# Dummy TensorE products around the first expert unit, and a reordered square root in the tail, in an LSTM-step + MoE block

## The reference, cut to what matters

```python
def step(carry, xp_t):                       # 8 steps, one after the other
    h_prev, c_prev = carry
    g = xp_t + h_prev @ u                    # 512x128 @ 128x512
    gates = sigmoid(g[:, :3 * H]); c_cand = tanh(g[:, 3 * H:])
    ...
    c = fg * c_prev + ig * c_cand
    h = og * tanh(c)
...
x = layernorm(x + lstm(x))
logits = einsum('GSM,ME->GSE', x, router_w)          # 8 groups of 512 tokens, 8 experts
dispatch, combine = gating_top2(logits, C=128)
expert_inputs = einsum('GSEC,GSM->EGCM', dispatch, x)
hidden = gelu(expert_inputs @ w0) * (expert_inputs @ w1)   # 128 -> 688
expert_outputs = hidden @ wo                               # 688 -> 128
x = layernorm(x + einsum('EGCM,GSEC->GSM', expert_outputs, combine))
```

## Time and profile before

| what | value |
|---|---|
| median of 3 runs | 311.33 us (310.96 to 311.38) |
| the profiled execution's own time | 310.78 us |
| its span | 309.0 us |
| mean granted clock of TensorE | 0.979 |
| busy share of the span: PE, DVE, ACT, POOL | 91%, 83%, 69%, 57% |

### The profile page before, as it was taken

The page is one execution under the profiler, slowest core; times in us unless marked ns, Lnnn a source line. Parts: engine busy times, 40 slices in busy tenths (PEclk is TensorE's granted clock), DMA queues, the critical chain, the costliest instruction groups (busy, mean ns, idle before and its releaser), DMA issues.

```text
span 309.0 us, 5728 instructions
## 1 busy us (share of the span) xinstructions
PE 279.8 (91%) x1671; PEld 233.7 (76%) x1671; DVE 257.9 (83%) x816; ACT 213.5 (69%) x484; POOL 176.7 (57%) x148
## 2 busy tenths in 40 slices
PE   8999988975969999999999999999999999897840
PEld 8666555635968999999998787788888888787730
DVE  2789997899859998888888988988777678899975
ACT  4787865556687777776778687776655665564964
POOL 5011148878777787776878578827447265662400
PEclk9999999977999999999999999999999999999995
DMA  6996081724273227224454857524223135452444
GB/s 193 379 395 238 8 253 48 217 69 134 78 225 92 71 69 228 65 57 52 72 93 35 204 71 164 71 20 64 45 25 45 26 34 146 67 94 19 79 143 136
DMA packets 46109, 34.97 MB, mean 113 GB/s; under 512 B 6993, under 2 KB 40720, under 8 KB 46080
## 3 DMA queue, kind: packets, MB, share of 16 engines
q1 hardware_dynamic: 35392, 26.56, 28.9%
q0 software_dynamic: 10688, 8.07, 17.8%
HBM read 17.86 MB, written 17.10 MB: 113 GB/s over the span
## 4 chain that ended last, share of the span: by engine, by line
PE 60%; DVE 15%; issue 8%; ACT 8%; POOL 8%; POOLq 0%; ACTq 0%; DVEq 0%
PE big L617 10%; PE big L619 10%; PE big L618 10%; POOL slots L464 6%; PE b_xnt L633 3%; PE b_xnt L636 3%; PE b_xnt L634 3%; PE big L531 2%; PE b_ht L633 2%; PE b_ht L636 2%; PE b_ht L634 2%; PE b_rt L653 2%; PE b_ht L578 2%; DVE e_lo L977 2%; PE b_xt L573 2%
## 5 line engine op out<-in xcount | busy, mean ns | idle before, releaser
L791 ACT ACTIVATE act_g<-big 128x256 f32<-128x256 f32 (+1 forms) x144 | 65.1, 452 | 55.4 <-PE big L619 54.6
L617 PE MATMUL big<-x_hi,e_hi 128*128 128x256 f32 (+1 forms) x264 | 84.7, 321 | 1.2 <-DVE x_lo L1037 1.2
L618 PE MATMUL big<-x_hi,e_lo 128*128 128x256 f32 (+1 forms) x264 | 84.4, 320 | 0.0
L619 PE MATMUL big<-x_lo,e_hi 128*128 128x256 f32 (+1 forms) x264 | 84.4, 320 | 0.0
L464 POOL DMA_INDIRECT slots<-rows,slot_ix x64 | 66.9, 1046 | 24.1 <-issue 18.4
L474 POOL DMA_INDIRECT tokens<-contrib,token_ix x32 | 50.3, 1572 | 32.0 <-DVE token_ix L1063 17.0
L474 POOL DMA_INDIRECT tokens<-zero_rows,token_ix x28 | 44.9, 1603 | 27.1 <-DVE token_ix L1063 20.0
L617 PEld LDWEIGHTS big<-x_hi,e_hi 128*128 128x128 f32 x264 | 50.2, 190 | 5.2 <-issue 1.5
L619 PEld LDWEIGHTS big<-x_lo,e_hi 128*128 128x128 f32 x264 | 50.3, 191 | 3.9
L618 PEld LDWEIGHTS big<-x_hi,e_lo 128*128 128x128 f32 x264 | 50.1, 190 | 3.9
L531 PE MATMUL big<-h,u_half 128*128 128x512 f32 x56 | 27.3, 633 | 3.5 <-DVE h L1018 3.5
(11 more groups left out here) (207 smaller groups left out, 654.1 us busy)
## 6 DMA issues: line engine op xcount, KB each, us to landing
e_raw<-in_L_ffn_w_kernel_dram SPq DMA_DIRECT2D x16, 320.0 KB
slots<-zero_rows SPq DMA_DIRECT2D x8, 548.0 KB, 8.4
e_raw<-in_L_ffn_wo_kernel_dram SPq DMA_DIRECT2D x8, 320.0 KB
xd<-slots SPq DMA_DIRECT2D x16, 137.0 KB, 2.5
xd<-slots SPq DMA_DIRECT2D x8, 274.0 KB, 3.1
x<-in_L_attn_input_seq_dram SPq DMA_DIRECT2D x8, 256.0 KB, 4.5
tokens<-rows SPq DMA_DIRECT2D x8, 256.0 KB, 2.7
x<-tokens SPq DMA_DIRECT2D x8, 256.0 KB, 3.2
```

The lines of the kernel that those rows point to most:

```text
L617: pe.matmul(dst, e_hi[q][:, c0:c0 + m], xdt_hi[u % 2][:, 0:w], start=True, stop=False)
L618: pe.matmul(dst, e_lo[q][:, c0:c0 + m], xdt_hi[u % 2][:, 0:w], start=False, stop=False)
L619: mm = pe.matmul(dst, e_hi[q][:, c0:c0 + m], xdt_lo[u % 2][:, 0:w], start=False, stop=True)
L791: nc.scalar.activation(act0[n % RH][0:m, 0:w], pre(n, P)[0], ACT.Gelu_apprx_tanh).then_inc(gelu_ready, 1)
```

## The change

TensorE gets three runs of dummy products, which now take the bank that they write as an argument. Ten stand between `x_part(7)` and `h_part(7)`, into `b_xt`, after a wait for the DVE step that last read `b_xt`. Twelve stand between `places(2)` and `turn_xd(0)`, into `big[2]`, after ACT has read that bank. Ten more stand between `turn_xd(0)` and the first products of unit 0. In the tail ACT gets a square root of one column of the constant `eps`, ahead of `copy_y` of the last unit; `fin_sqrt(0)` moves ahead of the last three of the five late rows; and DVE does all five steps of root 0 ahead of `fin_add(0)` instead of behind the statistics of group 6.

```diff
-            def keep_warm(n):
+            def keep_warm(n, home):
                 for _ in range(n):
-                    pe.matmul(b_ht[:, 0:P], ones[:, :], ones[:, :], start=True, stop=True)
+                    pe.matmul(home[:, 0:P], ones[:, :], ones[:, :], start=True, stop=True)
...
-            keep_warm(12)
+            keep_warm(12, b_ht)
...
                 if s + 1 < S:
                     x_part(s + 1, range(2, 4))
+                if s == S - 2:
+                    pe.wait_ge(slot_step, AS * (GB - 1) + 2)
+                    keep_warm(10, b_xt)
+            pe.wait_ge(gate_read, gate_no(S - 1, 2))
+            keep_warm(12, big[2])
             turn_xd(0)
+            keep_warm(10, big[2])
...
             high_hid(NU - 1, NCH - 1)
+            nc.scalar.activation(root_p[:, 0, 0:1], eps[:, :], ACT.Sqrt)
             copy_y(NU - 1)
...
             last_y()
-            for n in LATE_ROWS:
+            for n in LATE_ROWS[:2]:
                 early_row(n)
-            for i in range(NB // 2):
-                fin_sqrt(i)
-                for g in range(HALF + GB * i, HALF + GB * (i + 1)):
-                    fin_rows(g)
+            fin_sqrt(0)
+            for n in LATE_ROWS[2:]:
+                early_row(n)
+            for g in range(HALF, LAST):
+                fin_rows(g)
+            fin_sqrt(1)
+            for g in range(LAST, S):
+                fin_rows(g)
...
             fin_argument(0)
+            for n in range(FT):
+                fin_root_step(0, n)
             for k in range(GB):
                 fin_add(k)
                 for t in range(T):
                     fin_stat(LAST + k, t)
-                if k == 0:
-                    for n in range(FT):
-                        fin_root_step(0, n)
```

## The result

| | before | changed |
|---|---|---|
| median of 20 runs | 312.0 us (310.96 to 313.67) | 310.06 us (309.42 to 310.91) |
| the profiled execution's own time | 310.78 us | 309.42 us |
| its span | 309.0 us | 307.7 us |
| granted clock | 0.979 | 0.99 |

The ratio of the changed kernel to the one before is 0.994, with a 95% interval of 0.9926 to 0.9955. Of 312.0 us that is 1.87 us less (1.40 to 2.31). The forecast of 310.07 us was met to 0.01 us, but not by its sum alone: the kernel before ran at 312.0 us beside it, not at 311.33, so the forecast change of -1.26 us was too small. The close match is luck: the median of before stood 0.67 us higher than in the forecast, and the difference of the medians, 1.94 us, was 0.68 us larger.

What follows compares the result with a forecast made beforehand. DVE, not PE, was taken to set the pace through the first slow stretch, with POOL capping unit 0's gain at 0.39 us. Head +0.14 and tail -1.40 took the median from 311.33 to 310.07 us, range 309.2 to 311.2.

Steps and rivals of the forecast that it cites:

- The clock: TensorE around `h_part(7)` and unit 0's first products: half rate for 3.9 and 3.6 us, to become 1.00 from 61 to 84 us.
- Rival (2): Ahead of unit 0, half clock still holds for 3.6 us from 70.0; head +1.74, time 311.7 us; 8%.
- The dummies' price: Each fp32 128x128 dummy product on TensorE costs 0.2425 us at full clock: 2.43 us for ten, 2.91 for twelve.
- rival (3): Dummy products on TensorE cost 0.218 us each; head -0.39 to -0.2 us, time 309.6 us; 22%.
- Ten before `h_part(7)` at nothing: `h_part(7)` takes 3.70 instead of 5.40 us, but DVE's queue and the `xd` DMA cover it, so no time change.
- Twelve and ten around `turn_xd(0)`: Ahead of unit 0: turn 0.6 us late at 72.9, first product 1.55 us late at 75.55, last ten 0.95 too long.
- Head +0.14 us: Dummies through unit 0 cost +0.14 us, estimated at DVE's `cell` and carried to the end; POOL's cap bounds it at -0.39.
- Tail -1.40 us: Early table load and root 0 ahead of `fin_add(0)` let root 1 begin at 302.37 against 303.77: -1.40 us.
- The lower bound of -1.54: In the tail, the largest gain allowed, -1.54 us, if the dummy square root delays nothing.
- Rival (4): In the tail, the table change costs more than its load: `copy_y` 1.5 us late, time 311.4 us; 5%.
- Rival (5): Every microsecond at half clock on TensorE comes back: 3.75 us more gain, time 306.3 us; 3%.
- The sum: Whole kernel: +0.14 and -1.40 take the profiled execution from 310.78 to 309.52 us, the median from 311.33 to 310.07.

## Why the prediction was right, point by point

**The clock.** Right. It reads 1.00 in each stretch. The prediction counted the whole of both stretches as half clock, 7.5 us; their means of 0.56 and 0.53 give 3.4 us at half clock in each, 6.8 us together. Rival (2) (the clock falls all the same) did not happen with all three runs in place, though PE did fall idle for 0.97 us ahead of `places`, as that rival said.

**The dummies' price.** The term was taken at 0.2425 us a product and measured 0.216 to 0.23; the lower bound of 0.218, worked out from the old warm-up as if it had run at half clock, was the better number. A record takes 0.218 us at the start and 0.108 to 0.115 us in the runs of dummies here, so the start ran at half clock, though the column reads 1.00 there. This was rival (3)'s condition. Its consequence did not follow: it gave a head of -0.39 to -0.2 us, and the head cost 0.25.

**Ten before `h_part(7)` at nothing.** The gain of 1.70 us on PE came (3.69 against 5.40 us, 1.71) and the cover held: `chosen` came 0.2 us sooner (69.24 us), and the DMA of `xd` let PE begin at 72.16 us in the kernel with the first ten and no dummies behind them, against 72.32 us. But the step had an effect that the sum didn't have. I costed it at nothing, and it is where the head's 0.25 us come from. Three scatters together take 0.88 us longer with it, because DVE's three steps of step 7 moved ahead of their starts. `power(7)` starts at 82.86 instead of 82.47 us, and the wait that I had read as POOL waiting for DVE turned into DVE waiting for POOL.

**Twelve and ten around `turn_xd(0)`.** Forecast: turn at 72.9, first product at 75.55 us. Measured: 72.62 and 75.00. The last run is too long by 1.1 us (`x_lo` ended at 73.88), forecast 0.95. `cell` came at 79.32 us, not at 79.69 + 0.14, since the dummies were cheaper.

**Head +0.14 us.** Measured +0.25 at `shift(7)`, +0.22 at `h_hi` (0.37 less the 0.15 from before the edits). The size is near by luck, for the reason is another: not a late unit 0 (`root_x` came sooner), but POOL's longer scatters.

**Tail -1.40 us.** The mechanism was right at each step, and the term was mis-sized: it measured -1.72. `copy_y` was to be 0.18 us late and was 1.84 us behind `h_hi` instead of 1.82, since the 128x1 square root takes 0.20 us instead of 0.30 and the next instruction begins 0.11 us into it. In the same way the two late rows take 0.77 us from start to start, not 0.81. `fin_add(1)` starts 6.64 us behind `h_hi`, before 7.66: -1.02 against the forecast -0.82. The reciprocal of root 1 began 2.44 us behind `fin_add(1)`, forecast 2.56. The lower bound of -1.54 was too high, because I had let the measured lengths stand end to end, where they overlap by about 0.1 us an instruction. By its own words (the dummy root delays nothing, so 0.18 us more than 1.40) the bound would have been -1.58.

**The drain of a table load.** The Trainium skill, "ScalarE: Activation LUTs", "What ACT_TABLE_LOAD costs", gives 1.38 us for it beside the load. The measurement decides against it here: the load begins at 293.77 us, 0.01 us behind the end of `h_hi` (293.34 + 0.42), and the root starts 1.30 us later. Rival (4) falls with it. What the same page gives for the load itself, 1.28 us, is what the trace has.

**Rival (5)** (all time at half clock comes back) falls too: the head gives back none of it. The Trainium skill, "TensorE: Matmul & The Clock Gate", "Terms", has the loss on PE right (5.40 - 3.69 = 1.71 us of `h_part(7)`; half of 3.4 us at half clock). But no engine that waited for PE there set the time.

**The sum.** In the profile: +0.22 (head), +0.15 (ahead of the edits), -1.72 (tail), together -1.35 of the 1.36 us measured between the two executions. The comparison of 20 runs each gives -1.87 us (-1.40 to -2.31), which holds -1.72 + 0.22 = -1.50. The forecast change of -1.26 lies outside it, for the most part by the tail's 0.32 us. The chances have a small slip: the forecast (54%), (3) and (5) make 0.79, and with some spread taken off that is less than the 0.80 given for faster.

## What to carry to other kernels

Before pricing a slow stretch of TensorE, read who is busy in it: in the first stretch at half clock DVE was busy 3.85 of 3.90 us and a DMA came behind it; in the second the dummies brought DVE's `root_x` 0.45 us sooner, and POOL's queue took that away. Some 1.7 us a piece on PE came to nothing. A function table's load is cheap to move into an idle time of ScalarE, and worth more when the wait behind it is reordered in the same edit (0.98 and 0.32 us alone, 1.72 together). Where DVE's work moves by a few tenths against a row of POOL's scatters, look for DVE instructions with both inputs in SBUF that now run as a scatter begins: in these traces each added what it had left to the scatter.

## What was unexpected of the hardware

**Scatters that lengthen.** A scatter of 0.97 us becomes 0.85 us plus what is left of DVE's running instruction with two SBUF inputs, in most of the 39 long ones counted above. The three at 69 to 73 us took 1.20 to 1.33 us in every kernel in which the first ten dummies stand, on both kinds of chip, and 0.97 to 1.02 us in those without them.

**Chips on which everything takes 46 us longer.** The changed kernel on such a chip, waits of ACT (waiting tile and what it waited for; us in total, times, longest us):

```profile
ACT act_g L797 <- remote: 32.1, 7, 10.6
...
ACT L797 <- remote: 5.1, 1, 5.1
...
ACT x_hi L756 <- remote: 3.4, 1, 3.4
```

The releaser "remote", one that the profile can't name, is not among the waits of the kernel before on the first chip; here it holds ACT for some 40 us, all between 71 and 166 us, with single waits of up to 10.6 us. It is there in every kernel traced on these chips, whichever part of the change it has, and the kernel before took the same 46 us more; so it is not the change's. What it waits for was not settled. It makes `x_hi` of unit 0 late in ten of the eleven traces, so dummies around unit 0 may be worth something else there: the same change read 1.0001 on such a chip and 0.994 on the first.
